# Third tile's seeds ahead of the first product, and its last points ahead of the fourth tile's first points, in the first round

## The reference

```python
logits = conv1x1(gn(x), coupler_w) + coupler_b
sel = softmax(logits, axis=1); sel = sel / sel.sum(axis=1, keepdims=True)
conv = conv3x3(gn(x), w)                      # 8 * 64 channels
conv = conv.reshape(b, 8, 64, h, w) + bias
out = x + einsum('bschw,bshw->bchw', conv, sel)
```

## Time and profile before

| | us |
|---|---|
| median of 3 runs | 350.68 |
| the profiled execution | 350.75 |
| its span, first to last instruction | 348.9 |
| PE busy | 326.7 (94%) |
| DVE busy | 286.2 (82%) |
| POOL busy | 229.4 (66%) |
| ACT busy | 93.8 (27%) |

### The profile page before, as it was taken

How to read it: one execution, slowest core, us unless ns; L and a number is a source line. 1 busy time by engine, 2 the same in 40 slices (tenths; PEclk the granted TensorE clock), 3 DMA queues, 4 the chain that set the end, 5 groups by cost and what they waited for, 6 DMA issues and landing times.

```text
span 348.9 us, 5537 instructions
## 1 busy us (share of the span) xinstructions
PE 326.7 (94%) x1730; PEld 156.0 (45%) x1730; DVE 286.2 (82%) x503; ACT 93.8 (27%) x131; POOL 229.4 (66%) x329
## 2 busy tenths in 40 slices
PE   8858679989999999999999999999999999999993
PEld 8824234434444344444544344444544344444441
DVE  2599999978689879987699699987699697777776
ACT  1657401144611201145521111155411111111110
POOL 4420079999994467999964667999874489533343
PEclk9996899999999999999999999999999999999998
DMA  6952979902993099105891199007950397002002
GB/s 187 213 115 46 266 155 218 204 0 61 239 238 85 2 240 220 27 0 154 190 253 27 42 230 212 1 0 195 181 109 0 78 241 170 0 9 61 0 0 68
DMA packets 30274, 41.30 MB, mean 118 GB/s; under 512 B 2160, under 2 KB 23280, under 8 KB 29872
## 3 DMA queue, kind: packets, MB, share of 16 engines
q1 hardware_dynamic: 29376, 37.49, 47.0%
q10 hardware_dynamic: 880, 3.58, 3.5%
HBM read 11.97 MB, written 4.72 MB: 48 GB/s over the span
## 4 chain that ended last, share of the span: by engine, by line
PE 59%; DVE 20%; POOL 11%; issue 6%; DMA 2%; DVEq 1%; POOLq 0%; SPq 0%
PE pair L375 35%; PE pair L387 12%; PE pair L383 9%; DVE high L707 3%; DVE pair L706 3%; DMA x_raw<-x 2%; DVE pair L690 2%; POOL quarter L1007 2%; PE w_bank L435 2%; DVE pair L692 2%; POOL v_pts L981 2%; POOL x_res L1000 1%; POOL v_tail L973 1%; POOL bias_part L995 1%; DVE half L715 1%
## 5 line engine op out<-in xcount | busy, mean ns | idle before, releaser
L375 PE MATMUL pair<-w_head,op 128*128 128x512 f16 x864 | 235.9, 382 | 12.1 <-DMA op<-v_tail 5.3
L375 PEld LDWEIGHTS pair<-w_head,op 128*128 128x128 f16 x864 | 83.3, 98 | 117.5 <-DVE half L715 10.5
L387 PE MATMUL pair<-w_tail,op 128*128 128x512 f16 x288 | 110.3, 383 | 0.0
L532 ACT ACTIVATE m_sb<-pair 128x512 f32<-128x512 f32 x72 | 42.9, 596 | 224.6 <-PE pair L387 223.7
L1007 POOL TENSOR_TENSOR quarter<-half 128x256 f32<-128x256 f32 x71 | 52.7, 742 | 66.6 <-DVE half L715 66.4
L706 DVE TENSOR_TENSOR pair<-pair,sel_now 128x512 f32<-128x512 f32 x71 | 49.5, 697 | 36.9 <-PE pair L387 36.2
L715 DVE TENSOR_TENSOR half<-pair,high 128x512 f32<-128x512 f32 x71 | 49.1, 692 | 9.5
L383 PE MATMUL pair<-w_tail,op_two 128*128 128x512 f16 x144 | 55.1, 383 | 0.0
L690 DVE TENSOR_TENSOR pair<-pair,m_sb 128x512 f32<-128x512 f32 x72 | 49.6, 688 | 0.0
L692 DVE TENSOR_TENSOR pair<-m_sb,pair 128x512 f32<-128x512 f32 x72 | 49.3, 685 | 0.0
L707 DVE TENSOR_TENSOR high<-pair,sel_now 128x512 f32<-128x512 f32 x71 | 48.3, 681 | 0.0
(11 more groups left out here) (96 smaller groups left out, 193.3 us busy)
## 6 DMA issues: line engine op xcount, KB each, us to landing
op<-v_head SPq DMA_DIRECT2D x14, 600.0 KB, 8.1
x_res<-x_pix SPq DMA_DIRECT2D x8, 576.0 KB, 6.6
op_two<-v_head SPq DMA_DIRECT2D x14, 300.0 KB, 9.2
op<-v_tail SPq DMA_DIRECT2D x14, 300.0 KB, 6.9
op<-v_head SPq DMA_DIRECT2D x14, 288.0 KB, 8.5
out<-y_out SPq DMA_DIRECT2D x7, 576.0 KB, 3.9
x_raw<-x ACTq DMA_DIRECT2D x3, 1152.0 KB, 10.6
w_raw<-weight SPq DMA_DIRECT2D x6, 384.0 KB, 11.5
```

Source lines behind the costliest of these rows:

```text
L375: nc.tensor.matmul(dst, op[b][:, 0, j, at + r * PW:at + r * PW + P], w_head[:, j, r, :], start=fresh and r == 0, stop=False, skip_group_ch ...
L387: return nc.tensor.matmul(dst, op[b][:, 1, j, at:at + P], w_tail[:, j, 0, :], start=False, stop=True, skip_group_check=True)
L532: act.activation(m1_sb[:, i % LOOK, :], pair[i % SETS_OF_BANKS][:, 0, :], ACT.Copy).then_inc(m1_copied, 1)
```

## The change

Two moves, both in the first round alone.

On VectorE, `seed(2, 0)` (both seeds of tile 3) stood behind tile 1's product and halving. It stands now ahead of `selection(0)`, and so ahead of the first product. To do that for one round, that round is written out ahead of the loop, and the loop runs from the second.

On TensorE, tile 3's last points stood behind tile 4's first points. They stand now ahead of them, right behind tile 2's last points.

```diff
@@ -417,7 +417,10 @@
             def round_(n, more, begin=False):
 
                 for i in range(TILES):
-                    last_points(i, n, begin)
+                    if not (begin and i == 2):
+                        last_points(i, n, begin)
+                    if begin and i == 1:
+                        last_points(2, n, begin)
                     if 0 < i < TILES - 2:
                         first_points(i + 2, n, begin and i + 2 == FIRST_TILES)
                     elif i >= TILES - 2 and more:
@@ -769,7 +772,7 @@
-            def round_(n, more):
+            def round_(n, more, begin=False):
                 for i in range(TILES):
                     if i == 0:
                         dve.wait_ge(sel_copied, n + 1)
@@ -806,7 +809,8 @@
                     if i + 2 < TILES:
-                        seed(i + 2, n)
+                        if not begin or i:
+                            seed(i + 2, n)
                     elif more:
                         seed(i + 2 - TILES, n + 1)
                 if more:
@@ -949,8 +953,10 @@
             seed(1, 0, (1,))
             invert_again(0)
             divide_again(0)
+            seed(2, 0)
             selection(0, sel_now_parts, sel_copied)
-            with dve.Fori(0, ROUNDS - 1) as n:
+            round_(0, True, True)
+            with dve.Fori(1, ROUNDS - 1) as n:
                 round_(n, True)
             round_(ROUNDS - 1, False)
```

## The result

The changed kernel takes 351.81 us, the median of seven runs (351.66 to 352.08), against 350.68 (350.5 to 350.99): 1.003 times as long, 95% interval 1.002 to 1.004. Its span is 350.0 us where it was 348.9. The forecast was 351.8 us, slower by 1.08. The loss of 1.13 us is 0.3% of the time, but it stands clear of the spread: the slowest of the seven runs before is 0.67 us faster than the fastest of the seven after.

The account below looks back on a forecast made before the run. TensorE is busy 94%, but the first round was taken as bound by weights, GpSimd's dense queue, `shift` and tile 9's seed. Seeds add 1.20 less a 0.12 bubble: 350.75 + 1.08 = 351.83, against the median 351.8; range 350.6 to 352.5.

Parts of the forecast that it names:

- The sum: Whole kernel: profiled 350.75 plus 1.08 gives 351.83; against the median 351.76, say 351.8 us.
- The chain: First round, 45.10 to 75.28: weights, GpSimd's queue, `shift`, a seed end last; late weights move TensorE at tile 9 by 1.08.
- The second guard: Next round's logits on TensorE wait at 92.79 for GpSimd's tails, idle 0.48; both waits would have to be relieved.
- TensorE's move: Tile 3's last points run 44.9 to 47.2; tile 4 starts about 48.5, gap about 1.3; 0.1 to 0.3 ahead at tile 7.
- a bound of 0.25: VectorE's first round written out: effect between -0.25 and +0.25 us, from the idle loop entry; taken as 0.
- The second rival: TensorE's clock falls in the longer wait ahead of tile 9, giving 353.5 us; chance 0.05.
- Its price of 1.68: Tile 1's last points lasted 4.01 us, the same block for tile 2 2.33, so a fallen clock costs 1.68 more.
- The condition: Ahead of tile 9: wait of about 1.9 us, shorter than gaps of 2.40 and 2.52, TensorE busy without break from 47.44.
- the 947 ns of the earlier trace: GpSimd's rows go from 719 to 947 ns, median 727; one at 947 allowed stretching of up to 0.2 us.

Follow-up runs that it names:

- the run with one SBUF input: Changed kernel with tile 3's seeds behind the weights, plus two unused additions there, each adding a PSUM bank and an SBUF tensor; 350.78 us.
- The relief: Last two of six `input_and_bias` moved behind tiles 11 and 14, in every round; on the unchanged kernel 351.0 us, on the changed kernel 349.47 us.
- the relieved kernel before: Unchanged kernel with the last two of six `input_and_bias` moved behind tiles 11 and 14; 351.0 us (349.43 to 353.2), ratio 0.9997.

## Why the prediction was right

*The time.* 351.8 was forecast, 351.81 measured. The sum had one term, and it was measured three times: 1.08 on VectorE's step, 1.07 at the ends of the rounds, 1.1 in the times. That the two agree to 0.01 is luck, as the seven runs spread over 0.42; that they agree to 0.1 is not.

*The chain.* The step that carried the argument was to ask who else waits for `sel_now`. That GpSimd's queue passes the lag on is shown: moving the weights without the seeds costs it, moving the products without the weights doesn't, and giving that queue 3.6 us takes the loss away. (The description of the kernel says that three queues wait for the weights. There are three waits in two queues: L775 on VectorE, L990 and L1069 on GpSimd.)

*The second guard.* That the logits would stop any gain at tile 9 is shown by the run with `shift` made short: TensorE waits no more at tile 9, and the logits start at 92.71 (92.79 before).

*TensorE's move.* The block ran from 44.87 as forecast (44.9), tile 4's first points started at 48.25 (48.5), the gap behind it was 1.04 (1.3). I had left out of those two that the loop's entry goes, though I had it as a bound of 0.25. It was worth nothing, as forecast. TensorE was 0.26 us ahead at tile 7 (59.59), within the 0.1 to 0.3 (with the entry, 0.12 + 0.25 would have made the upper end 0.4).

*The clock.* The second rival, at 0.05, did not take place in the changed kernel: the clock was 1.00 behind the wait of 1.93. Its price of 1.68 is near what falls cost elsewhere (1.32, 1.45 and 1.68), but its working was not sound: tile 1's last points took 4.01 us with the fallen clock, and they also take 3.68 with the clock at 1.00 (38.18 to 41.86 in the run with one SBUF input), since two of its matmuls then wait for VectorE's `w_tail`. So that fall cost TensorE 0.33 us there, and nothing by tile 2, whose last points start at 42.4 to 42.8 in every trace. The condition was put wrongly as well. I argued from the length of the wait and from the busy time ahead of it, and the traces show that these do not decide it. In the run with `shift` made short the clock fell behind the 1.82 us, shorter than the 1.93, with TensorE busy without a break from 48 to it. The same gap of 2.40 at 38 was followed by 0.50 in 40 to 42 in the kernel before, and by 1.00 in VectorE's move alone and in the run with one SBUF input. Idle times of 2.56 and 3.38 us were followed by a fall, one of 2.04 was not. The Trainium skill ("TensorE: Matmul & The Clock Gate", Part 1) says that the clock is set by how busy the array has been of late. The traces agree in so far as the same gap of 2.52 us was followed by a fall in one execution and by none in another, so the gap alone does not decide it; no run here shows what does.

*What I missed.* Below GpSimd's queue lay 1.3 us that the kernel could win. The relief opens it, and TensorE's move makes it come in eleven of twelve runs where the relief alone has it in three. And I took the 947 ns of the earlier trace rows for a spread that might come anywhere. It has a place and a cause: rows of 0.94 to 0.95 us stand at 102.91, 179.70 and 256.49, each beside an instruction of VectorE with two SBUF inputs (L650), of which there are none beside GpSimd's queue in the 26.90 us of the earlier trace rows (see the last section).

## What to carry to other kernels

Before moving work ahead of an instruction to fill a gap on the busiest engine, list everyone who waits for that instruction, and follow the one whose queue has no idle row: filling a gap is free only if the filler delays no dense queue that something waits for. A gap next to such a queue on another engine can be slack and not time to win, as here; relieve that queue first, then the order and even the gap's effect on the clock begin to count. Put the filler behind the result that others wait for, not ahead of it.

## What the runs showed of the hardware that was not expected

In these traces an instruction of VectorE with two SBUF inputs does not run beside one of GpSimd that reads SBUF. `shift`, one element for each partition, took 1.77 us and 1.87 us and ended with GpSimd's instruction each time (74.61 and 74.59 in the kernel before, 75.63 and 75.60 in the change); in the relieved kernel before it took 0.28, as it started later, and ended with it again (72.56 and 72.55). With one input tensor it took 0.21. Two additions of 512 columns with two SBUF inputs took 2.37 us beside GpSimd's work and 1.28 with GpSimd idle; with one input from PSUM they took 1.28 beside it. GpSimd is held too: 1.63 and 1.41 us for rows of 1.28 and 1.15. The kernel before shows it in the softmax for the next round, where GpSimd's row is the second to start and takes 0.70 for its usual 0.46:

```profile
107.61 0.46 DVE L662 TENSOR_TENSOR logit<-mix,total 128x288 f32<-128x288 f32 x1
```

```profile
107.69 0.70 POOL L1011 TENSOR_TENSOR mixed<-quarter 128x128 f32<-128x128 f32 x1
```

By the Trainium skill ("SBUF — State Buffer", the section "SBUF: two separate sides") the two engines share a pair of ports as an exclusive lock, which a VectorE instruction with two SBUF inputs needs against a GpSimd instruction that reads SBUF, and the one that starts second waits; the traces agree for all these rows.

A fall of the clock can cost nothing. The kernel before was at 0.50 in 40 to 42 and took 350.75; the run with one SBUF input had 1.00 in every stretch from 38 to 58 and took 350.80. And the fall is hardly seen in the mean granted clock of an execution: it was 0.980 in the profile of the relieved kernel before, where the clock fell in 48 to 52 as well, and 0.981 in that of the kernel before, where it did not. It takes the granted clock by stretch to see it. By the two groups of its times the relieved kernel before had that fall in nine of twelve runs; only one of them was profiled.
